# A mixture-of-experts kernel on one core: SyncE's weight stream with at most two halves under way

## The chip, the cores and the metric

The kernel runs on one NeuronCore of one Trainium2 chip. The metric is the device time of one execution in microseconds (us), as the median of several runs; lower is better. One execution was also taken by the hardware profiler, and all rows below come from it.

## The reference, cut to what matters

Two layers act on `x` (8 batches of 100 tokens, 512 wide), with a context of 722 rows per batch. The first is a gated product with the context; the second sends each of the 800 tokens to one of 16 experts.

```python
xl = layernorm(x)
x1 = einsum('eth,efh->etf', xl, ctx)
x  = x + einsum('etf,efh->eth', gelu_tanh(x1) * x1, ctx)

h = layernorm(x).reshape(-1, 512)
logits = h @ router_w                      # 16 experts
assign = argmax(logits)                    # one expert for a token
g = sigmoid(logits[assign])
hh = gelu(h @ w1[assign] + b1[assign])     # w1: 16 x 512 x 1024
y = hh @ w2[assign] + b2[assign]           # w2: 16 x 1024 x 512
out = x + y * g
```

All is float32. The weights of one expert are 2 MiB of `w1` and 2 MiB of `w2`, 64 MiB for the 16.

## The kernel before, in words

Every engine has its own instruction stream, written by hand with semaphores. There are two phases.

The first (to about 145 us) walks the 8 batches. It computes the context product, normalises the tokens, finds each token's expert and rank there, and scatters the token's row (its 512 values with gate, mean and inverse deviation, cut into four quarters of 131 floats) into the tensor `rows` in HBM, in which each expert has its own stretch. SyncE loads context and tokens meanwhile, and in between the 16 halves of the weights of experts 0 to 3 (`load_weights`, L230 and L267).

The second phase works in units of 32 tokens of one expert. The number of units of an expert is known only at run time; with these inputs there are 31: 3, 1, 2, 5, 1, 1, 1, 2, 1, 3, 1, 2, 2, 2, 3, 1 for experts 0 to 15. Four weight slots (`SLOTS`) lie in SBUF, expert e in slot e modulo 4. For unit j the engines do this:

- ScalarE (ACT, L482 to L490) applies the gelu of unit j (L487), then waits until the rows of unit j+2 have landed, says so with `s_land` (L489), and issues the load of the rows of unit j+4 (`load_unit`, L203 to L207; the profile shows it as `area<-rows`, L205 reads the place, L206 is the transfer). These transfers go through ScalarE's own DMA queue, q10 in the profile. One moves 32 rows in four quarters: 128 pieces of 524 bytes, laid out so that the access pattern's slowest dimension is the quarter (4).
- VectorE normalises the landed rows (L638), TensorE transposes them (L395), VectorE copies them out (L643), TensorE multiplies by `w1` (`first_layer`, L376), VectorE transposes and adds the bias (L648, L655), ScalarE applies the gelu (L487), TensorE multiplies by `w2` (`second_layer`, L387), VectorE adds the rest (L669), and GpSimd scatters the result to `out` (L775).
- TensorE's order is first layer of unit j+1, transposition of unit j+2, second layer of unit j. So the gelu of unit j+1, which needs the second layer of unit j, waits for the rows of unit j+2.
- SyncE (L271 to L282) refills the slots for experts 4 to 15: 12 experts, 48 halves of 1 MiB (128 partitions of 8 KiB each, `load_half`, L223 to L225), on its own queue, q1. It waits until the first layer of the last unit of the slot's old expert is done (`s_hp`), issues both halves of `w1`, waits for that unit's second layer (`s_y`), and issues both halves of `w2`. Nothing there asks whether earlier halves have landed, so as many halves can be queued as slots are free.
- A half's landing raises its own semaphore (`s_w1[slot][h]`, `s_w2[slot][h]`) by 16. TensorE waits for it at L373 and L385.

Of the kernel before, what the change touches and what calls it, by code (L numbers as in the profile page):

```python
# [81 lines left out]
def build(nc, x, ctx_main, ctx_rest, ctxT_a, ctxT_b, router, w1, b1, w2, b2, consts, out):  # L82
# [5 lines left out]
    with ExitStack() as stack:  # L88
# [3 lines left out]
        def sem(name):  # L92
            return stack.enter_context(nc.semaphore(name))

        def sems(name, n):
            return [sem(f"{name}{i}") for i in range(n)]
# [75 lines left out]
        s_w1, s_w2 = ([sems(f"{n}_{i}_", 2) for i in range(SLOTS)] for n in ("s_w1", "s_w2"))  # L172
# [20 lines left out]
        s_next = sem("s_next")  # L193
        s_prep, s_yo, s_at_out, s_y_free = sem("s_prep"), sem("s_yo"), sem("s_at_out"), sem("s_y_free")
        s_done = sems("s_done", 2)
        s_apart_v, s_apart_p, s_apart_a, s_apart_t = (sem(f"s_apart_{n}") for n in "vpat")

        block = stack.enter_context(nc.Block())

# [9 lines left out]
        @block.sync  # L209
        def _(sp):  # L210
            def load_x(b):
                sp.dma_start(xin[:, b % 3, :], x[b]).then_inc(s_x[b % 3], 16)

            def load_ctx(b):
                r = b % 2
                sp.dma_start(cxs[r][:, 0:SC - 1, :], ctx_main[b]).then_inc(s_ctx[r], 16)
                sp.dma_start(cxs[r][0:REST, SC - 1, :], ctx_rest[b, 0:REST]).then_inc(s_ctx[r], 16)
                sp.dma_start(cxs[r][REST:CW[-1], SC - 1, :], ctx_rest[b, REST:CW[-1]]).then_inc(s_ctx[r], 16)

            def load_ctxT(b, part):  # L220
                sp.dma_start(ctxTs[b % 2][part], (ctxT_a, ctxT_b)[part][b]).then_inc(s_ctxT[b % 2][part], 16)

            def load_half(dst, src, signals, h):  # L223
                n = dst.shape[1] // 2
                sp.dma_start(dst[:, n * h:n * h + n], src[:, n * h:n * h + n]).then_inc(signals[h], 16)  # L225

            early_weights = iter([(W[:, e], w[e], signal[e], h) for e in range(SLOTS)
                                  for W, w, signal in ((W1, w1, s_w1), (W2, w2, s_w2)) for h in range(2)])

            def load_weights(n):  # L230
                for _ in range(n):
                    load_half(*next(early_weights))

            sp.dma_start(con[:, 0:C_ONE], consts[:, 0:C_ONE]).then_inc(s_con0, 16)
            load_x(0)
            load_ctxT(0, 0)
            load_ctxT(0, 1)
            load_ctx(0)
            sp.dma_start(con[:, C_ONE:C_ALL], consts[:, C_ONE:C_ALL]).then_inc(s_conl, 16)
            sp.dma_start(rw[:, :, :], router).then_inc(s_rw, 16)  # L240
            load_x(1)
            load_ctxT(1, 0)
            load_ctxT(1, 1)
            load_ctx(1)
            sp.wait_ge(s_no_tokv, 1)
            sp.dma_start(tok_at, no_tok).then_inc(s_no_tok, 16)
            load_x(2)
            for b in range(NB):
                if b + 2 < NB:
                    for part in range(2):  # L250
                        sp.wait_ge(s_x1ps[part], b + 1)
                        load_ctxT(b + 2, part)
                if b == 2:
                    sp.dma_start(b1s[:, :, :], b1).then_inc(s_b1, 16)
                load_weights(EARLY[b])
                if b + 2 < NB:
                    sp.wait_ge(s_att, b + 1)
                    load_ctx(b + 2)
                if b + 3 < NB:
                    sp.wait_ge(s_x2, b + 1)  # L260
                    load_x(b + 3)
                if b == NB - 2:
                    sp.wait_ge(s_x1ps[1], NB - 1)
                    sp.dma_start(b2q.rearrange("q (e d) -> q e d", e=E),
                                 b2.rearrange("e (q d) -> q e d", q=Q)).then_inc(s_b2, 16)
            sp.wait_ge(s_att, NB)
            load_weights(4 * SLOTS - sum(EARLY))  # L267


            sp.wait_ge(s_plan, 1)  # L270
            with sp.Fori(1, E // SLOTS) as g:  # L271
                for s in range(SLOTS):
                    before = sp.value_load(ends[0:1, bass.ds(SLOTS * g + (s - SLOTS), 1)],
                                           min_val=s + 1, max_val=MAXU)
                    one = bass.ds(SLOTS * g + s, 1)
                    first, second = (w[one].rearrange("o p k f -> (o p) k f") for w in (w1, w2))
                    sp.wait_ge(s_hp, before)
                    load_half(W1[:, s], first, s_w1[s], 0)
                    load_half(W1[:, s], first, s_w1[s], 1)
                    sp.wait_ge(s_y, before + 1)  # L280
                    load_half(W2[:, s], second, s_w2[s], 0)
                    load_half(W2[:, s], second, s_w2[s], 1)  # L282

        @block.tensor
# [534 lines left out]
```

## Time and profile before

| what | us |
|---|---|
| median of 3 runs (349.13 to 355.09) | 352.95 |
| the profiled execution's own time | 353.3 |
| its span, from the first to the last instruction | 351.4 |
| TensorE busy (matmuls) | 257.9 |
| VectorE busy | 121.5 |
| GpSimd busy | 75.4 |
| ScalarE busy | 35.1 |

The span is what the rows divide up; the execution's own time is 1.9 us longer. Busy times overlap, and TensorE runs at one of two clocks (2.4 GHz, shown as a granted clock of 1.00, and 1.2 GHz, shown as 0.50), so a long busy time may be a slow clock. The mean granted clock was 0.886.

### The profile page before, as it was taken

The page shows a single profiled execution, that of the slowest core. Times are in us where ns is not written, and L with a number is a line of the kernel's source. Part 1 is how long each engine was busy: PE and PEld are TensorE (multiplying, and loading weights), DVE is VectorE, ACT ScalarE, POOL GpSimd, SP SyncE. Part 2 cuts the span into 40 slices and gives each one's busy share as a digit, 9 for nine tenths or more (in the row PEclk, how much of TensorE's full clock was granted, in tenths as well). Part 3 has the DMA queues.
Part 4 walks back from the last instruction along what each step waited for, and adds up shares of the span by engine and source line. Part 5 has one row for each costly group of instructions (what it writes and reads, how often), then busy time and mean ns, then how long its engine had stood idle before and what let it go on. Part 6 is the DMA issues. An engine that isn't in the chain of part 4 may idle for free.

```text
span 351.4 us, 10028 instructions
## 1 busy us (share of the span) xinstructions
PE 257.9 (73%) x3660; PEld 183.5 (52%) x3661; DVE 121.5 (35%) x400; ACT 35.1 (10%) x81; POOL 75.4 (21%) x109
## 2 busy tenths in 40 slices
PE   1989898988989583499757979277654895589970
PEld 0956756747758250266445756144542673456750
DVE  3134543535434462154222544112221342234520
ACT  1202101011011002110000000000000000000010
POOL 1001404314223243022201222111011122022221
PEclk9999999999999855599967999865786899699996
DMA  7999789898999596129998179999999589970110
GB/s 260 363 338 325 265 312 339 316 337 296 415 389 398 216 400 232 49 65 358 414 398 291 34 268 355 401 400 400 380 387 349 177 329 415 366 280 28 27 34 15
DMA packets 22362, 100.36 MB, mean 286 GB/s; under 512 B 3312, under 2 KB 8400, under 8 KB 13128
## 3 DMA queue, kind: packets, MB, share of 16 engines
q1 hardware_dynamic: 15044, 93.02, 69.9%
q0 software_dynamic: 2368, 4.40, 3.4%
q10 hardware_dynamic: 4932, 2.70, 2.8%
q8 instruction: 12, 0.20, 0.2%
q14 instruction: 6, 0.05, 0.0%
HBM read 95.58 MB, written 4.97 MB: 286 GB/s over the span
## 4 chain that ended last, share of the span: by engine, by line
DMA 32%; issue 26%; PE 24%; POOL 6%; DVE 4%; ACTq 2%; DVEq 1%; SPq 1%; ACT 1%; POOLq 0%
DMA area<-rows 27%; PE bank L387 10%; PE bank L376 10%; DMA xs<-in_x 3%; POOL rows L717 2%; DMA rows<-nothing,pad_at 2%; POOL tok_at L726 2%; PE bank L309 1%; PE bank L395 1%; POOL rs_x L710 1%; ACTq L205 1%; POOL row L710 1%; DVE area L638 1%; DVEq L651 1%; ACTq L206 1%
## 5 line engine op out<-in xcount | busy, mean ns | idle before, releaser
L387 PE MATMUL bank<-W,area 128*32 128x128 f32 x1984 | 74.9, 308 | 3.9 <-issue 3.1
L376 PE MATMUL bank<-W,area 128*32 128x256 f32 x992 | 67.5, 415 | 11.8 <-issue 11.2
L387 PEld LDWEIGHTS bank<-W,area 128*32 128x32 f32 x1984 | 62.9, 124 | 10.9 <-issue 5.7
L775 POOL DMA_INDIRECT out<-area,at_out x32 | 31.4, 982 | 150.3 <-DVE area L669 149.3
L376 PEld LDWEIGHTS bank<-W,area 128*32 128x32 f32 x992 | 37.1, 120 | 32.9 <-issue 21.7
L302 PEld LDWEIGHTS bank<-xnT,area 128*128 128x128 f32 (+1 forms) x384 | 45.1, 195 | 4.8 <-issue 4.8
L302 PE MATMUL bank<-xnT,area 128*128 128x100 f32 (+1 forms) x384 | 45.2, 281 | 1.0 <-ACT xnT L426 1.0
L309 PE MATMUL bank<-area,hidT 128*100 128x512 f32 (+1 forms) x96 | 45.6, 601 | 0.0
L395 PE MATMUL bank<-con,area 128*128 128x128 f32 x32 | 11.1, 345 | 44.8 <-DVE area L638 44.8
L395 PEld LDWEIGHTS bank<-con,area 128*128 128x128 f32 x32 | 4.7, 147 | 60.3 <-issue 60.3
L638 DVE TENSOR_SCALAR area<-area 128x128 f32 (+1 forms) x32 | 11.4, 355 | 65.0 <-ACTq L489 50.3
L487 ACT ACTIVATE area<-area 128x256 f32<-128x256 f32 x32 | 13.3, 416 | 187.5 <-PE bank L387 143.4
L669 DVE SCALAR_TENSOR_TENSOR area<-bank,area 128x128 f32 x31 | 10.9, 351 | 38.9 <-PE bank L387 36.0
L710 POOL TENSOR_TENSOR row<-ve_t,con 100x4 f32<-100x4 f32 x8 | 8.2, 1027 | 72.3 <-DVE ve_t L505 72.3
L648 DVE STREAM_TRANSPOSE area<-bank 128x256 f32<-128x256 f32 x31 | 14.0, 450 | 24.0 <-PE bank L376 22.1
L309 PEld LDWEIGHTS bank<-area,hidT 128*100 128x100 f32 (+1 forms) x96 | 14.3, 167 | 13.7 <-issue 13.7
L655 DVE TENSOR_TENSOR area<-area,b1s 128x256 f32<-128x256 f32 x31 | 13.3, 428 | 15.2 <-issue 14.8
L288 PE MATMUL bank<-con,xs 100*128 100x100 f32 x32 | 4.8, 278 | 17.2 <-DVE xs L507 17.2
L432 ACT ACTIVATE hidT<-bank 128x300 f32<-128x300 f32 x16 | 6.7, 420 | 64.8 <-PE bank L302 60.7
L288 PEld LDWEIGHTS bank<-con,xs 100*128 100x128 f32 x32 | 3.2, 151 | 18.1 <-DVE xs L507 11.3
L717 POOL DMA_INDIRECT rows<-row,pos x8 | 10.1, 1269 | 5.6 <-DVE pos L559 4.1
L659 DVE SCALAR_TENSOR_TENSOR area<-xs,area (+1 forms) x31 | 10.8, 348 | 0.0
(83 smaller groups left out, 157.9 us busy)
## 6 DMA issues: line engine op xcount, KB each, us to landing
W<-in_w SPq DMA_DIRECT2D x64, 1024.0 KB, 11.7
area<-in_ctx_main SPq DMA_DIRECT2D x8, 1280.0 KB
area<-in_ctxT_a SPq DMA_DIRECT2D x8, 768.0 KB, 8.4
area<-in_ctxT_b SPq DMA_DIRECT2D x8, 676.0 KB, 7.7
area<-rows ACTq DMA_DIRECT2D x36, 65.5 KB
xs<-in_x SPq DMA_DIRECT2D x8, 200.0 KB
area<-in_ctx_rest SPq DMA_DIRECT2D x8, 160.0 KB
out<-area,at_out POOLq DMA_INDIRECT x32
```

Source lines behind the costliest of these rows:

```text
L302: last = nc.tensor.matmul((p_xa, p_xb)[part][0:n, T * c:T * c + T], ctxTs[b % 2][part][:, k, P * c:P * c + n], xnT[:, k, :], start=(k == 0 ...
L309: last = nc.tensor.matmul(p_att[0:T, :], hidT[0:CW[c], c, :], cxs[b % 2][0:CW[c], c, :], start=(c == 0), stop=(c == SC - 1))
L376: last = nc.tensor.matmul(p_h[U * q:U * q + U, 0:FQ], curT[:, U * k:U * k + U], mine, start=(k == 0), stop=(k == KD - 1), tile_position=(0 ...
L387: last = nc.tensor.matmul(p_y[U * q:U * q + U, 0:DQ], hT[:, U * c:U * c + U], W2[:, slot, c, DQ * q:DQ * q + DQ], start=(c == 0), stop=(c ...
L395: nc.tensor.transpose(p_blk[:, 0:P], cur, ident).then_inc(s_blk, 1)
L487: nc.scalar.activation(hT, h_pre, ACT.Gelu).then_inc(s_act, 1)
L638: nc.vector.tensor_scalar(cur, mine[:, 0:DQ], mine[:, DQ + 1:DQ + 2], mine[:, DQ + 2:XW], ALU.subtract, ALU.mult).then_inc(s_next, 1)
L648: nc.vector.transpose(h_pre, p_h[:, 0:FQ]).then_inc(s_hT, 1)
L655: nc.vector.tensor_tensor(view, view, bias.unsqueeze(3).to_broadcast([P, 2, Q, U]), ALU.add).then_inc(s_hb, 1)
L710: nc.gpsimd.tensor_tensor(rs, ve, neg_half.to_broadcast(list(rs.shape)), ALU.pow).then_inc(s_rs, 1)
L717: nc.gpsimd.indirect_dma_start(rows, bass.IndirectOffsetOnAxis(ap=pos[b % 2][:, :], axis=0), row[:, b % 2, :], None, bounds_check=last_row ...
L775: nc.gpsimd.indirect_dma_start(out_q, bass.IndirectOffsetOnAxis(ap=at_out[r][:, :], axis=0), y_out[:, r, :], None, bounds_check=last_out, ...
```

## The change

Only SyncE's loop in the second phase changes. Before each half is issued, SyncE now also waits until the half two places ahead of it in the stream has landed: the first half of `w1` of a slot waits for the first half of `w2` of the slot before, the second for the second, and the two halves of `w2` wait for those of `w1` of their own slot. The semaphore increments on `s_apart_s` stand between two waits so that each is an instruction of its own; nobody waits for them.

```diff
             with sp.Fori(1, E // SLOTS) as g:
+                loaded, past = sp.snap(16 * g + 16), sp.snap(16 * g)
                 for s in range(SLOTS):
...
                     sp.wait_ge(s_hp, before)
+                    sp.sem_inc(s_apart_s, 1)
+
+                    prior = past if s == 0 else loaded
+                    sp.wait_ge(s_w2[s - 1][0], prior)
+                    sp.sem_inc(s_apart_s, 1)
                     load_half(W1[:, s], first, s_w1[s], 0)
+                    sp.wait_ge(s_w2[s - 1][1], prior)
+                    sp.sem_inc(s_apart_s, 1)
                     load_half(W1[:, s], first, s_w1[s], 1)
                     sp.wait_ge(s_y, before + 1)
+                    sp.sem_inc(s_apart_s, 1)
+                    sp.wait_ge(s_w1[s][0], loaded)
+                    sp.sem_inc(s_apart_s, 1)
                     load_half(W2[:, s], second, s_w2[s], 0)
+                    sp.wait_ge(s_w1[s][1], loaded)
+                    sp.sem_inc(s_apart_s, 1)
                     load_half(W2[:, s], second, s_w2[s], 1)
```

No transfer changes its place, its size or its queue. What stands on SyncE for one slot (slot 1; `L273` reads the unit count `ends`) was this before:

```order
L225 ISA [waits s_hp]
L225 DMA W<-in_w 128x2048
L225 ISA
L225 DMA W<-in_w 128x2048
L280 REGISTER_ALU
L225 DMA W<-in_w 128x2048 [waits s_y]
L225 DMA W<-in_w 128x2048
```

and is this now (line numbers are those of the changed file):

```order
L225 ISA [waits s_hp,s_w2_0_0]
L225 DMA W<-in_w 128x2048
L225 ISA [waits s_w2_0_1]
L225 DMA W<-in_w 128x2048
L288 REGISTER_ALU
L225 DMA W<-in_w 128x2048 [waits s_y,s_w1_1_0]
L225 DMA W<-in_w 128x2048 [waits s_w1_1_1]
```

The four transfers are the same, in the same order; each has a wait of its own for the landing of another half in front of it.

## Rows read from the trace of the kernel before

**Rows 1.** us, then busy by engine, clock, DMA share and GB/s, by stretch.
```profile
193.00:203.00 10.00, 10.00 (x239) 7.33 (x231) 5.08 (x15) 1.15 (x3) 2.85 (x5) 1.00 0.11 32
211.00:269.00 58.00, 35.46 (x614) 24.40 (x614) 12.84 (x37) 2.53 (x7) 8.16 (x14) 0.78 0.99 388
278.00:315.00 37.00, 26.56 (x571) 19.55 (x562) 11.63 (x34) 2.50 (x6) 6.64 (x11) 0.91 0.91 357
315.00:351.00 36.00, 24.51 (x614) 18.47 (x613) 11.96 (x35) 2.91 (x7) 8.96 (x15) 0.93 0.10 28
```

**Rows 2.** Chain that ended last, shares of the span by engine.
```profile
DMA 32%; issue 26%; PE 24%; POOL 6%; DVE 4%; ACTq 2%; DVEq 1%; SPq 1%; ACT 1%; POOLq 0%
```

**Rows 3.** The same chain in order of time: start us, us, what.
```profile
168.55 19.40 DMA area<-rows
...
216.57 21.07 DMA area<-rows
...
238.84 19.56 DMA area<-rows
...
289.97 19.29 DMA area<-rows
```

**Rows 4.** ScalarE in order of time: start, us, instruction, idle before.
```profile
172.77 0.42 ACT L487 ACTIVATE area<-area 128x256 f32<-128x256 f32 x1 [5.08 <-PE bank L387]
...
200.85 0.42 ACT L487 ACTIVATE area<-area 128x256 f32<-128x256 f32 x1 [3.56 <-PE bank L387]
...
204.85 0.42 ACT L487 ACTIVATE area<-area 128x256 f32<-128x256 f32 x1 [3.59 <-PE bank L387]
206.13 1.07 ACTq L206 DMA_DIRECT2D area<-rows  x1
...
317.21 0.42 ACT L487 ACTIVATE area<-area 128x256 f32<-128x256 f32 x1 [4.20 <-DVE area L655]
...
339.76 1.07 ACTq L206 DMA_DIRECT2D area<-rows  x1
342.29 0.42 ACT L487 ACTIVATE area<-area 128x256 f32<-128x256 f32 x1 [3.39 <-DVEq L701]
```

**Rows 5.** Tile W: issue to landing of a half, all 64 halves.
```profile
DMA to landing us min/median/max: 5.2/11.7/22.8
```

**Rows 6.** Tile W: the same for 8 halves issued from 218 to 239.
```profile
DMA to landing us min/median/max: 18.1/19.6/22.8
```

**Rows 7.** DMA queues, 226.3 to 236.8: kind, packets, MB, share.
```profile
q1 hardware_dynamic: 566, 4.13, 98.6%
q10 hardware_dynamic: 131, 0.07, 2.4%
```

**Rows 8.** DMA queues, 341.0 to 342.8 (no weight packet there).
```profile
q10 hardware_dynamic: 132, 0.07, 14.8%
```

**Rows 9.** DMA queues, 206.1 to 209.7 (no packet of q10 there).
```profile
q1 hardware_dynamic: 193, 1.38, 91.0%
```

**Rows 10.** DMA queues, 209.7 to 211.1.
```profile
q10 hardware_dynamic: 132, 0.07, 16.2%
q1 hardware_dynamic: 11, 0.03, 5.8%
```

**Rows 11.** SyncE's queue in order of time, 165 to 200.
```profile
167.27 3.31 SPq L225 DMA_DIRECT2D W<-in_w  x4
184.11 0.81 SPq L225 DMA_DIRECT2D W<-in_w  x2
```

**Rows 12.** DMA queues, 182 to 184.
```profile
q10 hardware_dynamic: 25, 0.01, 2.5%
```

**Rows 13.** DMA queues, 186.0 to 187.2.
```profile
q1 hardware_dynamic: 44, 0.33, 75.4%
q10 hardware_dynamic: 118, 0.06, 17.3%
```

**Rows 14.** Tile W: issue to landing, second of the pair issued at 155.3.
```profile
DMA to landing us min/median/max: 7.4/7.4/7.4
```

More of the change, by code:

```diff
@@ L195, in build @@
         s_done = sems("s_done", 2)
-        s_apart_v, s_apart_p, s_apart_a, s_apart_t = (sem(f"s_apart_{n}") for n in "vpat")
+        s_apart_v, s_apart_p, s_apart_a, s_apart_t, s_apart_s = (sem(f"s_apart_{n}") for n in "vpats")
         block = stack.enter_context(nc.Block())
```

## The prediction

> **What bounds the kernel now.** I read the busy times by stretch first, then the chain that ended last, then ScalarE in order of time, then the DMA queues in short windows. The first phase, to about 145 us, is not touched. In the second phase the reader is to see three kinds of stretch [rows 1]. From 211 to 269 and from 278 to 315 the DMA engines are 0.99 and 0.91 busy at 388 and 357 GB/s. From 193 to 203 they are 0.11 busy while TensorE is busy all the time. From 315 on they are idle (0.10) and only computing is left.
>
> The chain says what the busy DMA engines hold up. 32% of the span is DMA [rows 2], and in order of time it is not weights: it is single loads of a unit's rows, 65 KB each, that take 16 to 21 us from issue to landing [rows 3]. Alone such a load is quick: its 132 packets (128 of data and one closing packet for each of four engines) pass in under 1.8 us [rows 8]. While they wait, units advance slowly; free of them, one gelu follows the other after 4.0 us (200.85, 204.85 [rows 4]).
>
> Behind them is the weight queue. A half takes 5.2 us from issue to landing at best, 11.7 in the median, and 18.1 to 22.8 where SyncE has issued most [rows 5, 6]. A half is 8 packets of 8 KiB on each of the 16 engines. From 226.3 to 236.8, 131 row packets pass while 566 weight packets do, 35 on each engine [rows 7]. If a row load lies on four engines, 33 packets each, that is one row packet per weight packet: a row load then costs as much time as four halves, some 10.4 us, and as ScalarE keeps two of them queued, its landing takes twice that.
>
> So two things share the second phase: the weights, and the units, held back by their rows. When rows crawl, slots are not freed, SyncE runs out of halves to issue (193 to 203), and at 315, with the last half landed, units remain: gelus from 317.21 to 342.29, then 9.1 us to the end of the span [rows 4]. This tail is what the crawl costs.
>
> **The change part by part.** *The waits themselves.* 12 slots get four landing waits each and six semaphore increments at most; SyncE computes nothing, and issuing a half takes it 0.4 us of every 2.6, so the instructions cost nothing. What can cost is that the queue runs dry. A half alone needs at least 5.2 us from issue to landing [rows 5]; with two under way that is one per 2.6 us, and moving 1 MiB at 388 to 400 GB/s takes 2.6 to 2.7 us [rows 1, 7]. So they just cover each other. I bound the price per half by 0 from below and by 0.6 us from above (the second half of a pair landed after 7.4 us [rows 14]; two such per pair would be 3.7 us, less what the row packets take anyway), and take 0.1: 48 x 0.1 = 5 us. Behind the waiting SyncE only later halves are queued, which TensorE needs four experts later.
>
> *What two halves do to the rows.* The question is whether a row packet still meets a weight packet each time. At the landing of half n, half n+1 still has its 8 packets per engine to go, and n+2 is issued only now. The trace shows that an engine takes weight packets in ahead of time. The row load issued at 206.13 [rows 4] came while two halves were under way. It has no packet until 209.7 [rows 9] (alone its first packet comes 1.4 us after issue: a load issued at 339.76 moves from 341.1 on [rows 4, 8]), and then all 132 pass in 1.4 us beside 11 weight packets [rows 10]. It waited 2.2 us, about 7 weight packets of 0.32 us, for what had been taken in, and then was not interleaved, since nothing more was queued. The second sign is at 184: SyncE issued nothing between 170.6 and 184.11 [rows 11], so the queue ran down to its last half. From 182 to 184 rows still pass at 12 packets per us [rows 12], from 186.0 to 187.2 at 98 per us, 118 packets, while weights flow [rows 13]. A short time in which no weight packet waited at the door let a whole row load in at once, although new halves were already issued.
>
> With two under way this door is open at every landing: about 7 or 8 of the next half's 8 packets are taken in, and n+2 arrives 1.0 us after its issue, some 1.2 us after the landing. At 98 packets per us a row load needs 1.3 us. So I expect a row load to cost: 1.4 us to arrive, on average half a cycle (1.4) to the next landing, 2.3 behind the packets taken in, 1.3 to pass, 0.5 to be seen: 7 us in place of 15 to 21. ScalarE has two queued and needs 1.2 us to issue one, so the rows allow a unit per (7 + 1.2) / 2 = 4.1 us, beside the 4.0 of computing.
>
> *A rule that speaks against it.* The rows show one row packet per weight packet in a full queue [rows 7]. The Trainium skill ("DMA: Bandwidth & Descriptors", section "Queues, rings and completion order") says that each DMA engine takes turns between the queues it has work for, a packet at a time, which agrees. Taken alone it speaks against this change: as long as one weight packet is queued, the turns are the same at two halves as at seven, and the time stays at 353. That result is the first rival below.
>
> *What is late next.* The weights. Their end now follows from the engines that also carry rows. Today the last half lands at 315, and the stream stood idle for 10 us (193 to 203 [rows 1]) and for about 3 more (275 to 278 and at 210). If units keep pace, these 13 us fill up; the four row loads that passed in them, 1.1 us each, move between the halves, +4; the waits cost 5. Last landing: 315 - 13 + 4 + 5 = 311. Units: the gelu at 172.77 is that of unit 5 [rows 4]; 26 more at 4.0 us end at 277, and at 4.9 us, with a low clock and waits of all kinds, at 300, so they are not the bound. Behind the last landing come the rest of the last second layer (2 us) and the same 9.1 us to the end of the span (342.29 [rows 4] to 351.4). Should units be behind by half a unit, 2 more: 311 + 2 + 9 + 2 = 324. With the 1.9 us around the span this is 326, against 353.3 for the profiled execution, which stands 0.3 above the median of the runs shown. Forecast: 326. Its own range is 315 (no price for the waits, rows always caught up) to 336 (units behind by two, 0.2 us per half more).
>
> **The rivals.** *One for one at any depth.* If the door is never open, because n+2 arrives before the last packet of n+1 is taken in (with rows taking turns only four packets may be in ahead, and 4 x 0.32 us is more than the 1.2), each row load still meets 32 weight packets. For it speaks the even pace of the full queue [rows 7], against it the burst [rows 12, 13], which came at the end of a half with another one issued. Time: no change, 350 to 356, say 353. A change that hardly binds, since SyncE's own waits come later, would give the same; against that stands the 18 us from issue to landing [rows 6], which is seven halves.
>
> *Half a door.* The door opens at some landings only, and a row load takes 10 to 13 us. Then (11.5 + 1.2) / 2 = 6.4 us per unit while weights flow, in place of about 9 now. Half of the tail's saving is lost: 336 to 346, say 341. For it: the margins above are tenths of a us.
>
> *The queue runs dry (slower).* Place: SyncE's wait before each half. If the landing, the wake-up, the issue and the first packet take longer under load than in an idle queue, a half takes up to 7.4 us instead of 5.2 [rows 14], which is 3.7 instead of 2.6 per half. If half of that is paid and rows still go one for one, the 36 halves that move in the two full stretches (95 us at 2.6) cost 36 x 0.55 = 20 us that nothing gives back: 373. It decides from a half's issue to landing above 6.5 us on average. Against it: 5.2 us in an idle queue, and a row load that meets an empty queue gets so much faster that the two conditions hardly hold together; some mixture at 360 to 367 is likelier, say 365. The Trainium skill (same page, section "Bandwidth") lists 6.15 us for a single transfer of 1 MB, issued from GpSimd; by it, as an estimate, two under way would give 3.1 us per half and the sum would be some 20 us worse. The trace here has 5.2 us for the same size from SyncE's queue, and that is used [rows 5].
>
> **How the numbers follow.** Forecast 0.58, half a door 0.16, one for one 0.18, dry queue 0.08. About 2% is what a measurement of this kernel can tell from no change (here 346 to 360). The forecast and half a door are faster by more than that (0.74); one for one is within it, with a little of the dry queue (0.19); the rest is slower (0.07). The range for 8 in 10 reaches from 314 to 354, to take in half a door and most of the one-for-one case.
>
> **What would show it.** In the profile of the changed kernel the issue to landing of a half should have a median near 6 us and no value above 9; the chain should hardly show row loads above 9 us; short windows in the full stretch should show bursts of q10 after each landing; the DMA share should be near 0.95 from 155 to about 311, without a hole at 193 to 203, and only one or two gelus should follow the last landing. Row loads still at 14 to 20 us would make the forecast wrong by the first rival, and a DMA share below 0.85 with longer intervals between landings by the last.

## The result, and the profile after

The changed kernel takes 333.2 us (median of 4 runs, 329.2 to 335.8) against 351.7 for the kernel before (349.1 to 355.1). The ratio is 0.942, with a 95% interval of 0.932 to 0.951. The ratio is that of the fast executions alone: of six executions of the changed kernel three took 329.2 to 331.1 us and three 335.7 to 337.2, and the profiled one, of 335.7 with a span of 333.9, is one of the slower three, so that its rows end some 5 us later than those of a faster one would. It is faster, as forecast; the forecast was 326.

The busy times by stretch of the changed kernel, to be held against [rows 1] (us, busy by engine, clock, DMA share, GB/s):

```profile
core 0: us, PE busy (x) PEld busy (x) DVE busy (x) ACT busy (x) POOL busy (x), PEclk, DMA share, GB/s
193.00:203.00 10.00, 8.02 (x194) 5.63 (x194) 3.69 (x11) 0.83 (x2) 2.82 (x5) 1.00 0.89 304
203.00:236.00 33.00, 20.35 (x473) 14.03 (x469) 10.47 (x31) 2.08 (x5) 6.45 (x12) 0.94 0.91 312
236.00:248.00 12.00, 11.59 (x211) 7.82 (x211) 4.03 (x12) 0.83 (x2) 1.24 (x3) 0.74 0.97 363
248.00:323.00 75.00, 52.84 (x1164) 35.62 (x1164) 23.63 (x70) 5.00 (x12) 15.16 (x26) 0.91 0.91 322
323.00:333.00 10.00, 1.29 (x32) 0.83 (x32) 0.35 (x1) 0.42 (x1) 0.98 (x1) 0.56 0.05 15
```

Two things changed places. The hole in the weight stream from 193 to 203 is filled (DMA share 0.89, was 0.11), and the tail without weights is 10 us, not 36. In exchange the stream is slower while it runs: 312 and 322 GB/s in its two long stretches, where the kernel before moved 388 and 357.

The chain that ended last, shares of the span by engine and by line, against [rows 2]:

```profile
DMA 52%; issue 25%; PE 8%; POOL 7%; DVE 3%; ACTq 1%; SPq 1%; ACT 1%; POOLq 0%; DVEq 0%
DMA W<-in_w 49%; POOL rows L730 2%; DMA rows<-nothing,pad_at 2%; PE bank L389 2%; POOL tok_at L739 2%; PE bank L322 2%; PE bank L315 1%; POOL rs_x L723 1%; PE bank L400 1%; DMA xs<-in_x 1%; POOL row L723 1%; DVE bn_x L514 1%; DVE xs L520 1%; SPq L225 0%; PE bank L330 0%
```

The 16 to 21 us row loads of [rows 3] are gone from it. What stands there is weights, link upon link. The last links of the same chain in order of time (start us, us, what):

```profile
308.96 6.14 DMA W<-in_w
...
315.24 8.15 DMA W<-in_w
323.39 0.04 issue
323.44 1.31 PE bank L400 x32
```

Each link is a half from its issue to its landing, then 0.1 to 0.2 us on SyncE, then the next but one half. SyncE's waits from 160 on say the same: 45 of them end with a landing and one, of 5.3 us, with a matmul, so the limit binds nearly everywhere. The last lands at 323.4, and after it only half of one second layer is left, and the way out.

Tile W of the changed kernel, issue to landing of the halves issued from 203 to 232 and from 236 to 245, against [rows 6]:

```profile
DMA to landing us min/median/max: 6.4/7.0/7.7
...
DMA to landing us min/median/max: 5.2/5.4/5.7
```

In the second stretch hardly a row load passes (none is issued between 229.2 and 243.6); in the first, ScalarE issues six. And the DMA queues of the changed kernel from 219.3 to 222.8, and then from 223.2 to 224.2, just behind the landing of a half at 222.6, with a row load issued at 220.14:

```profile
q1 hardware_dynamic: 152, 1.11, 87.0%
q0 software_dynamic: 32, 0.03, 3.0%
q10 hardware_dynamic: 11, 0.01, 0.5%
...
q1 hardware_dynamic: 16, 0.11, 51.8%
q10 hardware_dynamic: 62, 0.03, 10.7%
```

At this landing row packets come in a burst: 3 per us before it, 62 per us behind it, where the full queue of the kernel before let 12 per us pass all the time [rows 7]. It is one of the sharper ones. Counted over all 48 landings, 10 to 13 row packets per us pass in the first us behind a landing and 27 to 38 from 1.5 to 3.5 us behind it. By the packets in the trace, a row load of the second phase takes 3.6 to 10.5 us from issue to its last packet, mostly 5.5 to 9, while weights flow.

### The profile page after: what moved, and what is told of

Read it like the earlier page. It is cut to its first block, busy times and chain, and to the rows that moved or that the text cites. A ratio compares the mean times of both kernels' runs of the same rounds, so it can differ in the third digit from the quotient of the medians.

```text
span 333.9 us, 10106 instructions
## 1 busy us (share of the span) xinstructions
PE 248.4 (74%) x3660; PEld 172.3 (52%) x3661; DVE 120.3 (36%) x400; ACT 35.1 (11%) x81; POOL 75.0 (22%) x109
## 3 DMA queue, kind: packets, MB, share of 16 engines
q10 hardware_dynamic: 4932, 2.70, 2.8%
## 4 chain that ended last, share of the span: by engine, by line
DMA 52%; issue 25%; PE 8%; POOL 7%; DVE 3%; ACTq 1%; SPq 1%; ACT 1%; POOLq 0%; DVEq 0%
DMA W<-in_w 49%; POOL rows L730 2%; DMA rows<-nothing,pad_at 2%; PE bank L389 2%; POOL tok_at L739 2%; PE bank L322 2%; PE bank L315 1%; POOL rs_x L723 1%; PE bank L400 1%; DMA xs<-in_x 1%; POOL row L723 1%; DVE bn_x L514 1%; DVE xs L520 1%; SPq L225 0%; PE bank L330 0%
## 5 line engine op out<-in xcount | busy, mean ns | idle before, releaser
L389 PE MATMUL bank<-W,area 128*32 128x256 f32 x992 | 66.5, 407 | 32.2 <-DMA W<-in_w 21.4
L400 PE MATMUL bank<-W,area 128*32 128x128 f32 x1984 | 67.4, 290 | 7.0 <-DMA W<-in_w 4.7
L400 PEld LDWEIGHTS bank<-W,area 128*32 128x32 f32 x1984 | 56.6, 116 | 13.1 <-DMA W<-in_w 5.5
L389 PEld LDWEIGHTS bank<-W,area 128*32 128x32 f32 x992 | 33.2, 116 | 55.3 <-issue 28.8
L315 PEld LDWEIGHTS bank<-xnT,area 128*128 128x128 f32 (+1 forms) x384 | 44.3, 192 | 4.8 <-issue 4.8
L315 PE MATMUL bank<-xnT,area 128*128 128x100 f32 (+1 forms) x384 | 44.4, 278 | 1.1 <-issue 1.1
```

The costliest lines, as they stand in the source:

```text
L315: last = nc.tensor.matmul((p_xa, p_xb)[part][0:n, T * c:T * c + T], ctxTs[b % 2][part][:, k, P * c:P * c + n], xnT[:, k, :], start=(k == 0 ...
L389: last = nc.tensor.matmul(p_h[U * q:U * q + U, 0:FQ], curT[:, U * k:U * k + U], mine, start=(k == 0), stop=(k == KD - 1), tile_position=(0 ...
L400: last = nc.tensor.matmul(p_y[U * q:U * q + U, 0:DQ], hT[:, U * c:U * c + U], W2[:, slot, c, DQ * q:DQ * q + DQ], start=(c == 0), stop=(c ...
```

## The experiments

The theory behind the prediction, called A in most of what follows: on each DMA engine a row packet takes turns with weight packets that wait, so a row load pays for its 33 packets on its busiest engine; with two halves under way there are times in which no weight packet waits; the price is a weight stream that just about runs dry. B is the rival named in each expectation. The ratios below are to the kernel before, run on the same chip.

**How many halves are under way.** One, in place of two:

```diff
-                    sp.wait_ge(s_w2[s - 1][0], prior)
+                    sp.wait_ge(s_w2[s - 1][1], prior)
                     load_half(W1[:, s], first, s_w1[s], 0)
...
```

Each half waits for the one directly before it.

> Edit: each half waits for the half directly before it, so one is under way instead of two. Theory A (the price of the waits is the time from issue to landing of a half divided by how many are under way): a half alone takes 5.0 to 5.2 us from issue to landing and SyncE 0.2 us to issue the next, so 48 halves take 48 x 5.4 = 259 us; last landing near 413, time 420 to 430 us. Row loads are then quick (under 6 us). Rival B (SyncE's wait costs only the wake-up and the first packet, 1.2 us, and the rest of the 5.2 us is the moving): 48 x 3.9 = 187 us, time about 350 us.

429.4 us, ratio 1.215 (1.210 to 1.220). The chain is a half from issue to landing, time after time:

```profile
326.44 5.46 DMA W<-in_w
...
332.16 5.17 DMA W<-in_w
```

By the trace's landings, 47 intervals between the first and the last are 5.5 us in the mean, and row loads end 2.7 to 5.2 us after issue. So a half has a round trip of some 5.2 us, of which about 2.6 is moving 1 MiB; B, which took the rest to be hidden, is out. It also gives the stream's speed with two under way: 5.2 + 0.2, divided by two, is 2.7 us at best, and the stretch from 236 to 248 of the changed kernel comes to that: four halves land between 236.4 and 247.2.

Three under way:

```diff
-                    sp.wait_ge(s_w2[s - 1][0], prior)
+                    sp.wait_ge(s_w1[s - 1][1], prior)
                     load_half(W1[:, s], first, s_w1[s], 0)
...
```

Each half waits for the one three places ahead.

> Edit: each half waits for the half three places ahead, so three are under way. Theory A (a row load slips in only when the weight queue has nothing waiting at the engine's door, and with three under way 16 packets per engine are left at each landing, 8 more than are taken in ahead): row loads go one for one again, 15 to 20 us, and the time is that of the kernel before, 346 to 354 us. Rival B (a row load simply waits in proportion to how much weight is queued): row loads at about 9 to 11 us, less dry queue than with two, time 325 to 338 us.

354.3 us (349.7 to 356.3), 0.3% from the kernel before (353.2) and inside the spread of either. The row loads are back in its chain (start us, us, what), nearly to the figure of [rows 3]:

```profile
216.24 21.25 DMA area<-rows
238.69 19.45 DMA area<-rows
259.35 16.03 DMA area<-rows
```

From 226.7 to 236.7 its queues read as in [rows 7], though three halves are under way there and seven were before:

```profile
q1 hardware_dynamic: 544, 3.97, 99.7%
q10 hardware_dynamic: 125, 0.06, 2.5%
```

This is the sharpest result of the study. From 216 to 260, 12.5 row packets per us pass in the kernel before, 12.6 with three halves under way and 21.7 with two. Three halves or seven make no difference to a row load, and two make all of it; how much is queued does not count. Whether something always is can be read from the packets too: with three under way 15.6 weight packets are being moved at once in the mean of that stretch, nearly one on each of the 16 engines; in the changed kernel from 203 to 236 it is 13.5, and 12 or fewer for a quarter of the time. B, a share in proportion to the length, is out.

**What a row load pays for.** The same kernel as before, no landing waits, but the rows of a unit loaded as four quarters of 32 partitions (their semaphore then counts 64 in place of 16):

```diff
-            eng.dma_start(xr[:, at, :].rearrange("p o d -> p (o d)"),
-                          rows[bass.ds(col * U, U), :].rearrange("t (q d) -> q t d", q=Q)).then_inc(signal, 16)
+            for q in range(Q):
+                eng.dma_start(xr[U * q:U * q + U, at, :].rearrange("p o d -> p (o d)"),
+                              rows[bass.ds(col * U, U), XW * q:XW * q + XW]).then_inc(signal, 16)
```

> Edit: the kernel before, without SyncE's landing waits, but each row load is issued as four loads, one for each quarter (32 partitions of 524 bytes), so that its packets should lie on all 16 engines, 8 on each, instead of 32 on four. Theory A (a row load pays one weight packet for each of its packets on its busiest engine): it pays 8 x 0.32 = 2.6 us instead of 10.4; issue to landing 6 to 8 us in a full weight queue; the weights run at 2.7 us per half without a hole, last landing 285 to 295, time 300 to 318 us, faster than both kernels. Rival B (row loads are slow because the weight queue is long, whatever engines they lie on): time 345 to 355 us.

314.0 us, ratio 0.888 (0.884 to 0.892): much faster than both kernels, although a half now takes 21.7 us in the median from issue to landing. Queue q10 has 7092 packets in place of the 4932 on the page before: 60 more for each of 36 unit loads, which is 4 x 16 closing packets (the ones that raise the semaphore) instead of 4. So each quarter lies on 16 engines, and a unit's rows are 8 data packets on each rather than 32 on four. The Trainium skill ("DMA: Bandwidth & Descriptors", section "Why a DMA increments its semaphore by 16 and not by 1") gives the rule behind it: a transfer is split over the largest number of engines up to 16 that divides the slowest dimension of both sides. With 4 quarters that is 4, with 32 rows 16; the packet counts agree. Its busy times by stretch:

```profile
203.00:236.00 33.00, 29.21 (x708) 21.47 (x711) 14.86 (x44) 2.91 (x7) 8.22 (x14) 1.00 0.97 381
240.00:295.00 55.00, 44.03 (x954) 30.55 (x942) 19.56 (x59) 4.17 (x10) 10.87 (x21) 0.94 1.02 409
```

409 GB/s, and TensorE busy beside it: units and weights both run. B, by which the length of the queue slows the rows, is out. By the packets, a row load in the full queue takes mostly 7.3 to 8.3 us from issue to its last packet, much as in the changed kernel; what this run has on top of it is the faster stream. The last half lands at 300.3, not at the 285 to 295 expected: there is still a hole, from 192 to 199 the DMA share is 0.43 at 96 GB/s.

Then packet size. Each half issued as two pieces of 512 KiB, so that a weight packet has 4 KiB, and TensorE waiting for each piece:

```diff
-                n = dst.shape[1] // 2
+                n = dst.shape[1] // 4
                 sp.dma_start(dst[:, n * h:n * h + n], src[:, n * h:n * h + n]).then_inc(signals[h], 16)
```

> Edit: the kernel before, with each half of 1 MiB issued as two pieces of 512 KiB, so that a weight packet has 4 KiB instead of 8, and TensorE waiting piece by piece; no landing waits on SyncE. Theory A (one row packet passes for one weight packet, whatever its size): the four engines' 33 row packets now cost 33 x 0.16 = 5.3 us instead of 10.4, the row loads take 8 to 11 us, time 325 to 338 us. Rival B (the row load waits for the queued bytes, not for turns): nothing changes but TensorE's earlier start, 348 to 354 us.

332.2 us, ratio 0.944 (0.938 to 0.951). From 230 to 236 its queues show what a row load pays:

```profile
q1 hardware_dynamic: 595, 2.17, 95.3%
q10 hardware_dynamic: 129, 0.07, 4.0%
```

595 / 16 = 37 weight packets per engine pass beside about one row load's 132 packets (33 on each of four engines), as in [rows 7], in 6.0 us instead of 10.5. The turns are by packet, not by bytes. The Trainium skill's rule that the prediction weighed ("DMA: Bandwidth & Descriptors", section "Queues, rings and completion order": turns between queues at packet granularity) agrees at both sizes. What the page calls a packet is typically 9 to 17 of the single pieces that the profile counts as packets, and there the trace differs: in the 10.5 us of [rows 7] no tenth of a us has more than three row packets on the four engines, so a turn here is one piece. Halving the weight packets gave as much time as the change did. TensorE waits for smaller pieces in this run as well, which no run separates. The price is in the stream: 365 to 369 GB/s in its full stretches, where 8 KiB packets reach 388 to 409.

**What the change costs.** The changed kernel with rows on 16 engines:

> Edit: the changed kernel (two halves under way) with row loads in four quarters on all 16 engines as in the run before. It separates what sets the 3.5 us per half. Theory A (the four engines that carry rows land late and the other twelve idle meanwhile): with rows spread, a half takes 2.8 to 2.9 us, last landing near 295, time 305 to 318 us. Rival B (the time from landing to the next half's first packet leaves the queue dry at every half, rows or not): 3.3 to 3.5 us per half stay, time 325 to 333 us.

317.9 us, ratio 0.892 (0.888 to 0.897). The edit is the four-quarter load on top of the changed kernel. By the trace's landings a half takes 3.05 us in the mean (first landing 164.2, last 307.8), where the changed kernel takes 3.49 (159.6 to 323.4). A asked for 2.8 to 2.9, B for 3.3 to 3.5; it lies between, nearer to A. So most of the slow stream comes from rows that sit on four engines. Whether the rest is the limit itself is not shown: the profiled execution took 320.1 us, and two of the four took 314.0 and 315.7, as without a limit.

Four halves under way, rows on 16 engines (each half waits for the one four places ahead):

> Edit: row loads in four quarters on all 16 engines, and four halves under way. With two under way this took 318, with no limit 314 us. Theory A (with rows spread, the limit only costs, at most by a dry queue; four leave none): 312 to 316 us. Rival B (some part of the length of the queue still holds back rows or SyncE, whose issue takes 2 us each in a full queue): 305 to 311 us.

313.9 us, ratio 0.895 (0.888 to 0.902): the same as without any limit. Its last half lands at 300.6, 7 us before that of the run with two, whose profiled execution took 5 us more than its own faster ones. Once the rows are spread, no limit helps. What two cost is not told from nothing by the ratios (0.892 against 0.888 and 0.895); what is seen is the spread, 314.0 to 325.0 us with two and 312.7 to 316.6 with four.

Finally the margin. Two register loads, some 0.9 us, between each landing wait and the issue behind it, in the changed kernel:

```diff
                     sp.wait_ge(s_w2[s - 1][0], prior)
                     sp.sem_inc(s_apart_s, 1)
+                    sp.value_load(ends[0:1, bass.ds(SLOTS * g + (s - SLOTS), 1)], min_val=1, max_val=MAXU)
+                    sp.value_load(ends[0:1, bass.ds(SLOTS * g + (s - SLOTS), 1)], min_val=1, max_val=MAXU)
                     load_half(W1[:, s], first, s_w1[s], 0)
...
```

> Edit: the changed kernel (two halves under way), with two register loads, some 1 us in all, put on SyncE between each landing wait and the issue behind it. It measures how close the two halves are to just covering each other. Theory A (issue to landing of a half is 5.2 us at best, so two under way are at the edge with 2.7 us per half, and every delay is paid by half of it): 0.5 us more per half, 48 x 0.5 = 24 us, time about 355 us, which undoes the gain. Rival B (the next half still has 1.4 us of packets in the engines, so 1 us more is hidden): time 331 to 337 us, as the changed kernel.

353.2 us, ratio 0.999 (0.994 to 1.003): the gain is gone. 20 us more than the changed kernel is 0.42 us for each of 48 halves, half of the 0.9. One of its delays in the chain:

```profile
199.09 7.63 DMA W<-in_w
...
206.81 0.27 SPq L289
207.11 0.15 SPq L289
...
207.38 0.27 SPq L290
207.67 0.15 SPq L290
```

A holds: with two under way hardly anything of the round trip is in reserve.

**A miss.** Pieces of 512 KiB again, each waiting for the piece three places ahead, so that 1.5 MiB is under way in place of 2:

> Edit: the same pieces of 512 KiB with 4 KiB packets, and each piece waits for the piece three places ahead. At a landing two pieces, 16 packets of 4 KiB on each engine, are left. Theory A1 (an engine takes in some 64 KiB ahead, so all 16 packets are in and the door is open): row loads 5 to 7 us, with 1.4 to 1.5 us per piece, 96 pieces end at 295 to 305, time 308 to 320 us. Theory A2 (an engine takes in some 8 packets, whatever their size, so 8 are left outside and the door is shut): row loads as in the run with 4 KiB packets and no limit, 8 to 11 us, time as there or some us more.

357.9 us, ratio 1.019 (1.012 to 1.026), outside both. The rows did what A1 said and better: issue to last packet 4.3 to 7.3 us, against 9.5 to 12 with the same pieces and no limit. The stream did not. Tile W:

```profile
DMA to landing us min/median/max: 3.9/5.9/15.7
```

Half the bytes have a round trip of 3.9 us at best, not 2.6, and of 5.9 in the median; a third of that is the 1.94 us per piece that the landings show, 96 x 1.94 = 186 us. The expectation took 1.4 to 1.5 us per piece, from moving time alone. Its busy times say the same (275 and 287 GB/s):

```profile
203.00:236.00 33.00, 21.20 (x376) 12.28 (x368) 8.11 (x25) 1.67 (x4) 5.83 (x10) 0.78 0.84 275
240.00:295.00 55.00, 39.74 (x699) 24.15 (x699) 14.17 (x43) 2.92 (x7) 7.66 (x13) 0.76 0.85 287
```

## Why the prediction was right, and where it was off

- *Rows bound the second phase, and a row load pays one weight packet for each of its packets on four engines.* Right, and shown from three sides: spreading the rows over 16 engines (353 to 314), halving the weight packet (353 to 332), and no effect between three halves and seven.
- *With two halves under way row loads slip through, in about 7 us.* Right in size: the 27 loads issued from 161.7 to 314.9 took 6.7 us in the median from issue to last packet, where the prediction had 6.4 up to there. Its parts were off and made up for each other, which is luck. The first packet came 3.5 us after issue (5.1 said: 1.4 to arrive, 1.4 to the next landing, 2.3 behind the packets taken in), and the 132 packets then took 4.0 us (1.3 said); three of the 27 passed in 1.8 us or less. Most loads pass partly in turns and partly in a rush behind a landing, not as one burst. The first rival, one for one at any depth, is what happens at three; at two it is refuted by the time and by the 21.7 row packets per us.
- *Why they slip through.* The prediction said that an engine takes in 7 or 8 weight packets ahead of time, so that nothing waits at its door at a landing. The runs agree but don't prove it. With two under way the engines also run dry outright at times (13.5 weight packets moved at once in the mean, where three under way have 15.6), and that alone would let rows pass. Pieces of 4 KiB would tell the two apart, but in that run too the queue was often dry. This stays open: that engines are short of weight packets at moments with two under way, and hardly ever with three, is shown; whether packets taken in ahead matter beside it is not.
- *The waits cost 0.1 us per half, 5 us.* Not shown to be wrong. With rows spread, two under way end 7 us later than four (307.8 against 300.6), which is 0.15 per half; but 5 of the 7 us are what that execution took beyond the faster ones of its kernel, so the price of the limit alone lies somewhere from nothing to 0.15. The error is in the term for rows, "+4". I charged 1.1 us for the four loads that used to pass in idle time, and took the others to be paid in today's 315. But the half behind a landing is issued only when the slowest of 16 engines is done, and a row load lengthens the round trip: 7.0 us with rows against 5.4 without, in the two stretches above. Rows on four engines make the last landing 15.6 us later than rows on 16 (323.4 against 307.8). The semaphore of a half rises in 16 steps as the engines finish: in the changed kernel the twelfth comes 1.3 us before the last in the mean of 46 halves, 0.3 to 0.8 for those that landed from 238.8 to 250.5, where hardly a row load passed, 0.7 with rows on 16 engines, and 0.4 with one half under way. So the late engines hold up the next issue. That this lengthened round trip, and not the twelve engines' idle time as such, makes the whole 15.6 us is argued; no run separates them.
- *The sum.* Last landing: 311 said, 323.4 found. From there to the end of the span: 13 said, 10.5 found, since no unit was behind. So 324 became 333.9 in the profile, and 326 became 333.2 in the median. The mechanism was right, and the stream's speed was mis-sized, by 0.27 us in 3.22 per half in the profiled execution. That one took 5.0 us more than the median of the three faster ones (330.7); if these 5 us lie in the stream, the faster ones have 0.16 in place of 0.27, but none of them was profiled.
- *The dry queue as the slower rival.* It was priced at 365 and did not come, but it is near: 0.9 us more on SyncE takes the whole gain, and with a single half under way the time is 429. I had put its limit at 6.5 us from issue to landing. The halves take 7.0 with rows passing, and the kernel is still faster, because the rows did not stay slow at the same time: the pair of conditions that this rival needed does not occur together, as the prediction argued.
- *Half a door.* Three row loads do take 8.9 to 10.5 us, but they are the exception, and the chain holds none.
- *The signs.* Of the halves issued from 155 on the median from issue to landing is 6.9 us (near 6 said) and the longest 8.7 (none above 9 said). The DMA share is 0.92 from 155 to 323 (near 0.95 said), without the hole. One gelu follows the last landing, as said.

## What to carry to other kernels

When small loads on one queue crawl beside a stream on another, count packets on the busiest DMA engine, not bytes: here 65 KB on four engines cost as much time as 4 MiB of weights, and laying the same 65 KB over all 16 engines gave 11%, twice what throttling the stream gave. In this kernel a limit on the stream helped only where it was tight enough that the engines were short of weights at moments, and there it stood at the edge of running dry: a half cannot come sooner than its round trip divided by the number under way. Look at the round trip of one transfer (5.2 us here) before choosing that number.

## What the runs showed of the hardware

- With rows on four engines the effect of the limit is a step. One half under way: 429 us; two: 333; three and unlimited: 354 and 353.
- A 1 MiB load of 8 KiB packets has a round trip of 5.2 us with nothing else queued, a 512 KiB load of 4 KiB packets 3.9 at best: by these two some 2.6 us do not shrink with the size (the packets were halved along with it, which no run separates).
- SyncE's issue of a half is itself slow in a long queue. In the run with rows on 16 engines and no limit, SyncE's L226 (the issue) is 5% of the chain, in pieces like these. The run with four under way has less than 1% there and takes the same time (313.9 us both), so the slow issue cost nothing here:

```profile
237.39 1.74 SPq L226
239.23 2.46 SPq L226
```
